# Rotary products, GpSimd splits and half rows in another order in an attention stage

## The reference, cut to what matters

```
x = x + attn(cond(x))        # cond: x W^T + 0.5 (x A[label]) B^T
x = x + ffn(cond2(x))        # two projections with gated low-rank terms, top 2 of 8
# attn, for 32 sequences of 64 tokens, 32 query heads, 8 key heads, head size 32:
qkv = h @ w_qkv.T + b_qkv
q, k = rope(q), rope(k)      # out_r = xr*cos - xi*sin;  out_i = xr*sin + xi*cos
scores = where(causal, q k^T / sqrt(32), -1e20)
out = softmax(scores) v;  out @ w_o.T + b_o
```

## Time and profile before

| | us |
|---|---|
| median of 3 runs | 1141.48 (1140.61 to 1142.27) |
| the profiled execution's own time | 1139.95 |
| its span | 1138.1 |
| PE busy in the span | 1117.8 (98%) |
| DVE busy | 686.9 (60%) |
| ACT busy | 423.7 (37%) |
| POOL busy | 168.4 (15%) |

### The profile page before, as it was taken

One profiled execution on the slowest core, in us unless ns is written; L12 is line 12 of the kernel. 1 busy time (PEld: TensorE's weight loads), 2 busy tenths in 40 slices (PEclk: granted clock), 3 DMA queues, 4 the chain that ended last, 5 costly groups with the idle time before them and its releaser, 6 DMA issues.

```text
span 1138.1 us, 16858 instructions
## 1 busy us (share of the span) xinstructions
PE 1117.8 (98%) x6048; PEld 975.8 (86%) x6048; DVE 686.9 (60%) x1233; ACT 423.7 (37%) x1208; POOL 168.4 (15%) x134
## 2 busy tenths in 40 slices
PE   8999999999999999999989999999999999999998
PEld 6888888888888888888889998888888888888887
DVE  5312138888888888888896226133145776667664
ACT  5312125556565556655565124111122322222221
POOL 0000022333333333333242001000000000000000
PEclk9999999999999999999999999999999999999999
DMA  8020032222222233233255117374462223332112
GB/s 285 19 71 20 10 104 84 65 65 65 65 65 65 66 74 72 65 76 72 57 167 126 46 38 220 85 231 117 124 185 73 99 107 111 111 112 106 73 63 93
DMA packets 92900, 106.70 MB, mean 94 GB/s; under 512 B 8498, under 2 KB 74930, under 8 KB 92850
## 3 DMA queue, kind: packets, MB, share of 16 engines
q1 hardware_dynamic: 90146, 97.38, 28.2%
q0 software_dynamic: 2560, 8.39, 4.4%
q10 hardware_dynamic: 144, 0.26, 0.1%
HBM read 72.45 MB, written 25.17 MB: 86 GB/s over the span
## 4 chain that ended last, share of the span: by engine, by line
PE 85%; DVE 9%; issue 2%; ACT 2%; DMA 1%; DVEq 0%; SPq 0%
PE psum L958 17%; PE psum L1647 15%; PE psum L1955 14%; PE psum L280 13%; PE psum L1374 8%; PE psum L1935 4%; PE psum L2033 4%; PE psum L991 4%; DVE roped L774 2%; DVE rot_t L774 2%; PE psum L977 2%; DVE pt_l L779 2%; ACT pt_h L620 1%; PE psum L1039 1%; PE psum L1023 1%
## 5 line engine op out<-in xcount | busy, mean ns | idle before, releaser
L958 PE MATMUL psum<-p_h,c_high_low 128*128 128x512 f32 (+1 forms) x768 | 195.8, 361 | 0.5 <-DVE qkv L913 0.5
L958 PEld LDWEIGHTS psum<-p_h,c_high_low 128*128 128x128 f32 x768 | 132.3, 189 | 14.3 <-issue 0.7
L280 PE MATMUL psum<-c_high_low,w_h 128*128 128x512 f32 x384 | 119.8, 397 | 5.4 <-ACT c_high_low L215 5.4
L1647 PE MATMUL psum<-ring,rows 128*128 128x512 f32 x528 | 123.7, 392 | 1.1 <-DVE t_plain L1348 1.1
L1647 PEld LDWEIGHTS psum<-ring,rows 128*128 128x128 f32 x528 | 98.8, 188 | 23.9 <-DVE t_plain L1348 2.4
L1374 PE MATMUL psum<-chunk,rows 128*128 128x384 f32 (+1 forms) x576 | 108.0, 341 | 0.0
L958 PE MATMUL psum<-p_l,c_high_low 128*128 128x512 f32 (+1 forms) x384 | 102.8, 362 | 0.0
L1374 PEld LDWEIGHTS psum<-chunk,rows 128*128 128x128 f32 x576 | 101.4, 189 | 0.6 <-DVE qkv L913 0.3
L280 PEld LDWEIGHTS psum<-c_high_low,w_h 128*128 128x128 f32 x384 | 73.5, 192 | 22.2 <-ACT c_high_low L215 5.4
L715 POOL TENSOR_TENSOR c_high_low<-ring_plain,c_high_low 128x512 fp32r<-128x512 f32 x32 | 41.4, 1295 | 326.7 <-ACT c_high_low L589 187.7
L628 ACT ACTIVATE prob<-prob 128x64 f32<-128x64 f32 x240 | 57.8, 242 | 54.2 <-DVE prob L882 54.2
(11 more groups left out here) (174 smaller groups left out, 2181.0 us busy)
## 6 DMA issues: line engine op xcount, KB each, us to landing
ring_plain<-in_x_t SPq DMA_DIRECT2D x32, 256.0 KB, 3.0
ring_plain<-attn_scratch SPq DMA_DIRECT2D x32, 256.0 KB, 4.0
raw<-x_t_scratch SPq DMA_DIRECT2D x16, 512.0 KB, 4.1
rest<-in_b_base SPq DMA_DIRECT2D x16, 512.0 KB, 4.3
out<-rest SPq DMA_DIRECT2D x15, 512.0 KB, 2.9
ring_plain<-in_wqkv_t SPq DMA_DIRECT2D x10, 512.0 KB, 5.8
a_raw<-in_lora_a SPq DMA_DIRECT2D x32, 128.0 KB, 2.1
ring_plain<-ring_plain POOLq DMA_DIRECT2D x16, 256.0 KB, 3.5
```

The source lines that it names most:

```text
L280: mm = pe.matmul(to, stationary, moving, start=k == 0 and m == 0, stop=k == KT - 1 and last, skip_group_check=True)
L958: mm = pe.matmul(to, sx[:, kk, :], moving(w, n, kk), start=first, stop=False, skip_group_check=True)
L1647: mm = pe.matmul(self.psum[:, self.BANK_OF[i], :], w[:, cols], s, start=m == 0 and p == 0, stop=m == KT - 1 and p == 2, skip_group_check=True)
```

## The change

Four things move; no instruction is added or removed.

1. DVE, steps 1 to 15: the first of the four rotation products now stands ahead of `probs_low(w, 0)`; the other three, the subtraction and the addition follow it.
2. POOL, steps 1 to 15: `split_x(u, 1)` is taken out of the end of step u-1, and stands at the start of step u behind a new wait for the rotation of that step (`rotated >= 2v + 2`). `normalise(v, 1)` follows `split_a(u+1)` directly.
3. TensorE: `attend(w, 0)` and `transpose_p(w, 1)` stand ahead of part (1, 1) instead of (1, 0), so one part of four matmuls later.
4. POOL, step 16: the four `low_rest` of rows 0 to 3 move behind the normalisations: row 0 behind `normalise(v, 0)` and a wait for DVE's half of row 7, rows 1 to 3 behind `normalise(v, 1)`.

```diff
         def step(u, main, score, value, nxt):        # gpsimd
             v, w = u - 1, u - 2
+            if score and main:
+                pool.wait_ge(rotated, 2 * v + 2)
+                split_x(u, 1)
...
             if value:
                 add_low_values()
-            if score and not main:
-                fold2.low_rest(pool, 0)
             if score:
                 normalise(v, 0)
             if score and not main:
-                fold2.low_rest(pool, 1)
+                pool.wait_ge(fold2.last_row_low, 1)
+                fold2.low_rest(pool, 0)
             if nxt:
                 split_a(u + 1)
-                split_x(u + 1, 1)
             if score:
                 normalise(v, 1)
             if score and not main:
-                fold2.low_rest(pool, 2)
-                fold2.low_rest(pool, 3)
+                for k in range(1, fold2.RESTS):
+                    fold2.low_rest(pool, k)
...
+        def first_product(v):                        # vector
+            dve.wait_ge(qkv_out, v + 1)
+            dve.wait_ge(const_in, 16 * len(consts))
+            need(dve, rotated, 2 * v)
+            need(dve, qk_t, 3 * v)
+            real = products(0)
+            next(real)
+            return real
...
         def step(u, main, score, value, nxt):        # vector
             v, w = u - 1, u - 2
+            if score and main:
+                real = first_product(v)
             if value:
...
             if score:
-                dve.wait_ge(qkv_out, v + 1)
...
-                rotate(v, 0)
-                rotate(v, 1)
...
+                if not main:
+                    real = first_product(v)
+                rotate(v, real)
...
-        BESIDE = {(0, 0): [(transpose_p, 2, 0)], (1, 0): [(attend, 2, 0), (transpose_p, 2, 1)],
+        BESIDE = {(0, 0): [(transpose_p, 2, 0)], (1, 1): [(attend, 2, 0), (transpose_p, 2, 1)],
```

More of the change, by code:

```diff
@@ L769, in vector, with products, rotate @@
     def vector(dve):
-        def rotate(v, part):
+        def products(part):
             pairs = qkv[:, 0:QK].rearrange("p (h i two) -> p h i two", i=HD // 2, two=2)
             for n, (dst, table) in enumerate(((roped[:, :, :, part], (cos, sin)[part]), (rot_t[:, part, :, :], (sin, cos)[part]))):
-                last = dve.tensor_tensor(dst, pairs[:, :, :, n], table[:, :].unsqueeze(1).to_broadcast([P, NH, HD // 2]), ALU.mult)
-            last.then_inc((rot_re, rot_im)[part], 1)
+                yield dve.tensor_tensor(dst, pairs[:, :, :, n], table[:, :].unsqueeze(1).to_broadcast([P, NH, HD // 2]), ALU.mult)
+        def first_product(v):
[6 more added lines that the diff above has]
+            return real
+        def rotate(v, real):
+            next(real).then_inc(rot_re, 1)
+            *_, last = products(1)
+            last.then_inc(rot_im, 1)
+            dve.wait_ge(rot_re, v + 1)
+            dve.tensor_tensor(roped[:, :, :, 0], roped[:, :, :, 0], rot_t[:, 0, :, :], ALU.subtract).then_inc(rotated, 1)
+            dve.wait_ge(rot_im, v + 1)
+            dve.tensor_tensor(roped[:, :, :, 1], roped[:, :, :, 1], rot_t[:, 1, :, :], ALU.add).then_inc(rotated, 1)
         def probs_low(w, b):
@@ L823, in step @@
             if score:
-                dve.wait_ge(qkv_out, v + 1)
-                dve.wait_ge(const_in, 16 * len(consts))
-                need(dve, rotated, 2 * v)
-                need(dve, qk_t, 3 * v)
-                rotate(v, 0)
-                rotate(v, 1)
[L830 to L833, removed]
+                if not main:
+                    real = first_product(v)
+                rotate(v, real)
             if value and not score:
```

## The result

The changed kernel takes 1135.23 us (median of 5 runs, 1134.91 to 1136.48) against 1141.34 for the kernel before on the same chip: ratio 0.9948, 95% interval 0.9933 to 0.9962, so 6.1 us or 0.5% faster. The span of the profiled execution went from 1138.1 to 1133.1.

A forecast was written before the change was run, and what follows sets the result against it. TensorE, busy 98% of the span, was taken as the bound. The loop's 2.8 and the last unit's 2.5 made 5.3 off 1141.48, so 1136.2 us, range for 8 in 10 1132.0 to 1140.0.

The forecast's parts named there:

- TensorE's loss at `transpose_qk`: Loop steps: TensorE waits 0.54 a step for the second `pt_l`; 0.20 of it goes, 2.8 over fourteen steps.
- no more than that can be won in the loop: Loop: TensorE's wait at `transpose_qk`, 0.54 a step and 7.6 in all, was called the most that can be won.
- The product stands until 0.13 before POOL's end: Loop: DVE's moved rotation product, with two SBUF inputs, waits from 327.82 until 328.10, 0.13 before POOL's normalisation ends.
- the 4.54: Last unit: one DVE subtraction recorded with 4.54 instead of 1.25, read as standing until 0.13 before POOL's recorded end.
- the cover: Loop, DVE ahead of the product: four register waits taken at nothing, with room up to POOL's release at 328.10.
- The first rival: Loop: the product does not stand, 0.48 a step, 6.7; with 2.5 from the last unit 1132.3; chance 12%.
- the 1.92: Loop: earliest issue of DVE's product, put at 1.92 behind the first `qkv` instruction.
- Edit 3 covers 0.50 in `attend`: Loop: without the later `attend`, TensorE would wait 0.50 for the first `pt_l`; with it, cover of 0.24.
- The last unit, 2.46: Last unit: DVE's subtraction goes at 592.26 instead of 594.72, so 2.46 is won; bounds 1.2 and 2.5.
- The feared loss: Last unit: DVE lets one more POOL half row of 1.29 pass, leaving 1.2 of the 2.46.
- Behind it the same order follows, TensorE without pause, so what is won stays.: Behind the last unit's `pt_l` of sequence 0: the 2.46 won there is kept.
- The slower rival: Loop: the product stands longer than POOL's remainder, kernel slower from 0.66; at 0.81 1143.6; chance 5%.

The follow-up runs named there:

- e2: The kernel before with only POOL's `split_x` moved behind the rotation; 1140.97 us, ratio 1.0004 to the kernel before.
- e7: The changed kernel with POOL's second normalisation halved and DVE's two register values worked out before its wait for `qkv`; 1133.69 us, ratio 0.9929 to the kernel before.
- e1: The kernel before with DVE's product moved ahead and `attend` one part later, POOL's order untouched; 1155.28 us, ratio 1.013 to the kernel before.
- e6: The changed kernel with DVE's two register values worked out before its wait for `qkv`; 1135.98 us, ratio 0.9953 to the kernel before.
- e5: The changed kernel with POOL's second normalisation half as long in units 0 to 14; 1134.81 us, ratio 0.9942 to the kernel before.
- e4: The changed kernel with `attend` and the second `transpose_p` put back ahead of part (1, 0); 1136.95 us, ratio 0.9965 to the kernel before.
- e3: The kernel before with only POOL's `low_rest` half rows moved behind the normalisations in the last unit; 1138.38 us, ratio 0.9980 to the kernel before.
- e8: The changed kernel without POOL's wait for DVE's half row 7 ahead of `low_rest` row 0; 1136.09 us, ratio 0.9961 to the kernel before.

## Why the prediction was right

The forecast was 1136.2, the measured time 1135.23; the range held it.

1. *TensorE's loss at `transpose_qk`, 0.54 a step, of which 0.20 goes.* 0.21 went in each of the loop's steps, 3.0 in all where 2.8 were counted. e2 shows that POOL's new order alone shortens nothing. That "no more than that can be won in the loop" is not shown: e7's step is 26.34, and the second wait of the weight loads, 4.6 in all, was left out.
2. *The product stands until 0.13 before POOL's end.* Right to 0.01 in the changed kernel (326.48 against 326.61), and shown by e1, where the same product stands 1.3. (The 1.22 taken for the subtraction alone in the reading of the 4.54 is not the 1.25 of the earlier trace rows; it is what the instruction takes in the loop, 1.225 on average. By 1.25 the release would lie 0.16 before POOL's end.) The sum held, but for one of its two reasons only in part. It cost little because, as the text said, the cover reached to POOL's release; e6 shows that the release sets the time once that work is out of the way. The first rival, had its mechanism been true, would have given the 0.29 a step of e5 and not the 0.48 that I priced, since it too used the 1.92. Thus its price should have been 4.1 + 2.5, 1134.9, which is nearer to the measured 1135.23 than my forecast: the time alone doesn't tell the two apart. What decides for the mechanism of the forecast is e1, and e6, where the product takes 1.01.
3. *Edit 3 covers 0.50 in `attend`.* e4: a wait of 0.5 by the weight loads stands there without it. Its worth is 0.11 a step, because what TensorE waits there it need not wait at `transpose_qk`; the prediction gave no price for that.
4. *The last unit, 2.46.* 2.45 in the trace, up to the last `attend`. The subtraction 2.09, TensorE's pauses 0.79 and 0.85, where 2.1, 0.8 and 0.9 were foreseen, and the clock did stay at 1.00. The feared loss, DVE standing for a third half row of POOL, did not come: those two DVE instructions take 2.38 as before.
5. *"Behind it the same order follows, TensorE without pause, so what is won stays."* This step failed. Behind the last `attend` TensorE does pause: 1.0 of the 2.45 is lost again in the changed kernel, and 1.5 in e3, which has edit 4 alone. All seven kernels with the whole gain lose 1.0 to 1.9 there, and e8, with half of it, nothing (the table of marks). In the changed kernel 0.64 of it is the longer wait of TensorE in the output projection, with an ACT instruction ahead of it that is idle 0.92 for weight rows from a DMA where it was 0.17; in the others it is mostly a wait in the feed-forward. Why these waits grow is open. So the edits are worth 4.4 in the trace where 5.3 was forecast, and that the total came out close is in part luck: another 0.56 was gone ahead of attention, where nothing was edited, and the medians differ by 6.1 where the two spans differ by 5.0.
6. *The slower rival* needed a product that stands 0.66 or more. e1 is that case, brought about by POOL's work: it stood 1.31, and the kernel was 1.3% slower. The mechanism and its sign were right, and the price too: 0.48 of standing from 1.92 on is 0.29 from 2.11, so 1.31 costs 1.02 a step, 14.3 in all, and the loop of e1 is 14.3 longer between the marks. Only the changed kernel has no work on POOL to cause it.

## What to carry to other kernels

An instruction moved into idle time of one engine has to be laid beside what the other engines do at that moment: here the same move is worth 3 us or costs 14.5, by whether POOL has 1.24 us more queued. When a wait of the bound engine shrinks, ask for the next limit before pricing the rest: register work and POOL's release lay 0.08 apart, and the chain to `scores` had as little room as the one to `transpose_qk`. A wait that the result doesn't need can still change the time, as the one behind the normalisation, since it decides which engine's instruction comes first. And a gain in one stage has to be followed to the end of the kernel: of the 2.45 in the last unit, 1.0 to 1.9 was given back hundreds of microseconds later.

## What the runs showed of the hardware

A DVE instruction with two inputs in SBUF that is issued while POOL's runs is recorded from its issue, so it looks slow where it stands, and the idle column shows nothing: the product starts 1.99 behind the first `qkv` both in e6, where it stands and takes 1.01, and in e7, where it takes 0.83. Its recorded end less its length alone puts its true start 0.12 to 0.14 before the recorded end of POOL's instruction in six places: the earlier trace rows, the 4.54, the product and the 2.09 of the changed kernel, the 2.13 of e1 and the 3.30 of e8.

Who comes next was not decided by who was waiting. DVE waited in the 4.54 and in e8's 3.30, and POOL's next instruction passed it; in the earlier trace rows it waited for one instruction only and then got in, with more of POOL's behind. In the cases seen, DVE was passed where POOL's next instruction is recorded as starting well before the end of the one in front (588.80 against 588.96 in e8, 593.00 against 593.64 in the earlier trace rows), and got in where the two overlap by some 0.05. In both cases of the longer overlap POOL's DMA issues stood shortly ahead. That this is the rule is a reading of a few places, not shown by a run of its own.

A wait of DVE for its own preceding result is not free when register values have to be worked out behind it: 0.22 of idle time for two of them, against 0.11 (e6: 326.50 with `qkv` ending at 326.39) where they are worked out ahead.
